# First-layer weights of the small expert slots: read from four fixed buffers instead of from a place looked up at run time

## The reference

```
xn  = layernorm(x)
out = x + scan(xn) + moe(xn)

scan: g, v, d = xn @ Wg + bg, xn @ Wv + bv, xn @ Wd + bd
      h[t] = (0.001 + 0.998 * sigmoid(d[t])) * h[t-1] + sigmoid(g[t]) * tanh(v[t])

moe:  scores = sigmoid(xn @ Wg.T + bg + bias)           # 8 experts
      the two best experts of each token, weighted by their scores
      expert(e) = gelu(xn @ W1[e].T + b1[e]) @ W2[e].T + b2[e]   # 256 -> 1024 -> 256
      shared    = gelu(xn @ Ws1.T + bs1) @ Ws2.T + bs2            # every token
```

## Time and profile before

| | |
|---|---|
| median of the runs | 710.67 us (710.16 to 711.31) |
| the profiled execution: its time | 710.67 us |
| its span, first to last instruction | 708.8 us |
| PE, share of the span busy | 94% |
| PE without a gap, big slots | 345 to 620 us |
| small slots on PE | about 651 to 698 us |
| granted TensorE clock, mean | 0.99 of full speed |

### The profile page before, as it was taken

One profiled execution on the slowest core, in us unless ns is written; L12 is line 12 of the kernel. 1 busy time (PEld: TensorE's weight loads), 2 busy tenths in 40 slices (PEclk: granted clock), 3 DMA queues, 4 the chain that ended last, 5 costly groups with the idle time before them and its releaser, 6 DMA issues.

```text
span 708.8 us, 20193 instructions
## 1 busy us (share of the span) xinstructions
PE 665.5 (94%) x5872; PEld 521.3 (74%) x5873; DVE 513.5 (72%) x1329; ACT 430.4 (61%) x738; POOL 285.4 (40%) x261
## 2 busy tenths in 40 slices
PE   4879999999999999699999999999999999999993
PEld 3455747565656565488988888888888888898773
DVE  5878989898989888766667666676666666666652
ACT  7967776868686855455555555555555555555651
POOL 2132332323242424234554645545446455463421
PEclk9999999999999999999999999999999999999997
DMA  7424334342516131222433323334333243332421
GB/s 258 169 71 139 90 120 112 97 137 71 172 57 182 35 120 31 70 44 60 67 52 61 67 53 66 57 60 66 55 60 66 53 67 54 61 65 50 72 40 23
DMA packets 54172, 57.55 MB, mean 81 GB/s; under 512 B 13204, under 2 KB 48916, under 8 KB 54136
## 3 DMA queue, kind: packets, MB, share of 16 engines
q1 hardware_dynamic: 38456, 38.42, 18.4%
q0 software_dynamic: 15680, 18.69, 16.4%
HBM read 38.53 MB, written 18.55 MB: 81 GB/s over the span
## 4 chain that ended last, share of the span: by engine, by line
PE 75%; DVE 13%; issue 5%; ACT 3%; DMA 2%; POOL 0%; DVEq 0%; SPq 0%; ACTq 0%; POOLq 0%
PE bank L1213 33%; PE bank L1205 29%; PE bank L1232 3%; PE bank L1193 3%; PE bank L1262 2%; PE bank L1244 2%; DVE W L800 2%; DVE arena L896 1%; DVE arena L839 1%; DVE arena L897 1%; PE bank L1184 1%; DVE arena L852 1%; DVE small L809 1%; DMA arena<-in_gates 1%; PE bank L1149 1%
## 5 line engine op out<-in xcount | busy, mean ns | idle before, releaser
L1213 PE MATMUL bank<-W,arena 128*128 (+1 forms) x2304 | 305.8, 274 | 16.0 <-DVE arena L897 14.0
L1205 PE MATMUL bank<-rows,W 128*128 128x256 f16 (+1 forms) x1920 | 299.2, 294 | 0.3 <-issue 0.2
L1213 PEld LDWEIGHTS bank<-W,arena 128*128 128x128 f16 x2304 | 222.4, 98 | 58.0 <-DVE arena L897 20.4
L1205 PEld LDWEIGHTS bank<-rows,W 128*128 (+1 forms) x1920 | 186.2, 98 | 54.5 <-issue 0.8
L592 ACT ACTIVATE arena<-bank,par 128x256 f32<-128x256 f32 x256 | 134.0, 559 | 80.3 <-PE bank L1205 69.3
L502 POOL DMA_INDIRECT out<-arena,slot_add x64 | 109.7, 1714 | 146.4 <-ACT arena L729 136.6
L896 DVE TENSOR_SCALAR arena<-arena,par 128x256 f16<-128x256 f32 x284 | 101.7, 358 | 81.7 <-ACT arena L592 54.8
L897 DVE SCALAR_TENSOR_TENSOR arena<-arena,par 128x256 f16<-128x256 f32 x284 | 138.7, 488 | 10.1
L438 POOL DMA_INDIRECT lists<-entry,place x64 | 67.9, 1061 | 150.6 <-ACT arena L578 73.2
L487 POOL DMA_INDIRECT rows<-xhl_rows,slot_list x64 | 68.9, 1076 | 51.8 <-DMA slot_list<-lists 34.8
L600 ACT ACTIVATE rows<-bank 128x1024 f16<-128x1024 f16 x32 | 32.7, 1023 | 60.9 <-PE bank L1262 33.4
(11 more groups left out here) (157 smaller groups left out, 519.9 us busy)
## 6 DMA issues: line engine op xcount, KB each, us to landing
stage<-in_w SPq DMA_DIRECT2D x32, 512.0 KB
b2row<-in_b SPq DMA_DIRECT2D x39, 128.0 KB
arena<-in_x SPq DMA_DIRECT2D x8, 512.0 KB
xhl_rows<-W SPq DMA_DIRECT2D x8, 512.0 KB
out<-arena SPq DMA_DIRECT2D x8, 512.0 KB
W<-in_w SPq DMA_DIRECT2D x4, 512.0 KB, 9.3
lists<-entry,place POOLq DMA_INDIRECT x64
rows<-xhl_rows,slot_list POOLq DMA_INDIRECT x64
```

The source lines that it names most:

```text
L1205: ins = T.matmul(bank_, weights(w, wp * HALF + c * H + j * P, P), rhs[:, 2 * xp + c, :], start=n == 0, stop=n == 3 * KD - 1)
L1213: ins = T.matmul(banks[t // 2][:, (t % 2) * D:(t % 2 + 1) * D], h[:, hp, t * P:(t + 1) * P], weights(w, (2 + wp) * HALF + j * D, D), start ...
```

## The change

SP copies the first layer's weights (both halves, 8 KB in each of 128 partitions, 1 MB) of each small slot from `W` to one of four buffers within SBUF: the two `stage` buffers and two pieces of `arena`. The seven copies go to the buffers in turn. The first four are started by SP after its work on slots 28 to 31; the other three after its work on slots 32, 33 and 34, each when PE has ended the first layer of the small slot that used the buffer before. `pair1` takes its weights from these buffers, whose addresses are fixed numbers; before its first matmuls of a slot it waits for the copy. `pair2` and the big slots are as they were.

```diff
+        small_w1 = [h[:, :].bitcast(F16) for h in (stage[0], stage[1], arena[:, 3072:5120], arena[:, 5120:7168])]
...
+        w1_in = [sem(f"w1_in{i}") for i in range(DEEP)]
...
+            def small_weights(m):
+
+                if m == 0:
+                    for l in range(2):
+                        for part in range(2):
+                            sp.wait_ge(stage_used[l][part], NW)
+                    sp.wait_ge(r_ok, 2 * SEQS)
+                    sp.wait_ge(o_out, 16 * SEQS)
+                if m >= DEEP:
+                    sp.wait_ge(ev_ps, EV_B + (m - DEEP + 1) * PAIRS)
+                s = sp.value_load(slot_set[0:1, BIG + m:BIG + m + 1], min_val=0, max_val=NW - 1)
+                sp.dma_start(small_w1[m % DEEP], W[:, bass.ds(s * WSET, 2 * HALF)]).then_inc(w1_in[m % DEEP], 16)
...
                 slot(n, n % 2)
                 if n < BIG - 8 + SMALL:
                     early_list(n + 8)
+                if n >= BIG - DEEP:
+                    small_weights(n - (BIG - DEEP))
             for n in range(BIG, SLOTS):
                 slot(n, n % 2)
+                if n + DEEP < SLOTS:
+                    small_weights(n - BIG + DEEP)
...
-            def pair1(ev, k, rhs, w):
-
-                pe.wait_ge(ev_act, ev + 1)
+            def pair1(m, k):
+
+                pe.wait_ge(ev_act, EV_B + m * PAIRS + k + 1)
+                if k == 0:
+                    pe.wait_ge(w1_in[m % DEEP], m // DEEP * 16 + 16)
                 for jj in range(2):
                     for n in range(3 * KD):
                         c, (wp, xp) = n // 3, PASSES[n % 3]
-                        ins = T.matmul(ps_e[k][:, jj * SROWS:(jj + 1) * SROWS],
-                                       weights(w, wp * HALF + c * H + (2 * k + jj) * P, P), rhs[:, 2 * xp + c, :],
-                                       start=n == 0, stop=n == 3 * KD - 1)
+                        o = wp * HALF + c * H + (2 * k + jj) * P
+                        ins = T.matmul(ps_e[k][:, jj * SROWS:(jj + 1) * SROWS], small_w1[m % DEEP][:, o:o + P],
+                                       xgT_small[m % DEEP][:, 2 * xp + c, :], start=n == 0, stop=n == 3 * KD - 1)
                 ins.then_inc(ev_ps, 1)
```

More of the change, by code:

```diff
@@ L1267, in first_layer @@
                 if is_small(n):
-                    pair1(EV_B + (n - BIG) * PAIRS + i, i, xgT_small[(n - BIG) % DEEP], w)
+                    pair1(n - BIG, i)
                 else:
```

## The result

The changed kernel takes 705.42 us, the median of four runs between 704.81 and 706.30, against 710.94 (710.16 to 711.31) for the kernel before beside it: a ratio of 0.9925, 95% interval 0.9908 to 0.9942. Measured again later beside other kernels it takes 705.01 us, a ratio of 0.9916 (0.9904 to 0.9929). The forecast was 705.1 in a range of 702.0 to 710.0. The profiled execution has a span of 703.8 us against 708.8.

What follows compares the result with a forecast made beforehand. PE bounds the kernel, in small slots through its sequencer's address instructions. Terms: -8.1 (addresses) + 0.4 (last addition) + 1.8 (copies in big slots) + 0.3 (bias row) = -5.6 from 710.67, so 705.1 us, range 702.0 to 710.0.

Steps and rivals of the forecast that it cites:

- Address instructions: In small slots 33 to 38, removing pair1's eight address instructions takes PE's work from 39.83 to 31.69 us, 8.1 us less.
- my bounds of 6.4 and 8.9: Gain in small slots 33 to 38: 6.4 us with idle gaps at slot starts as before, 8.9 with none.
- Rival 5: In small slots, pair1's pace stays because something other than address instructions sets it: 713.2 us, chance 0.05.
- rival 4: PE's sequencer spaces fixed-address matmuls at 67 ns, so pair1 in small slots takes 0.80 us: 707.8 us, chance 0.05.
- rival 3: The chain of gelu, split and scales look-up, not PE, sets small slots at 6.2 us or more: 707.6 us, chance 0.10.
- The last addition: At the kernel's end, slot 37's addition ends later against PE's end: 0.4 us lost, between 0 and 0.5.
- The copies in big slots: Lists queued behind copies delay gathers, so PE stands still at the turnings of slots 29 to 31: 1.8 us lost.
- D = 4.4 us: Assumed time for one 1.05 MB copy within SBUF, near the mean of 2.6 and 6.2 us.
- my own formula: PE's stall at turnings: D - 3.4 for slot 29, D - 4.0 each for slots 30 and 31, D being copy time.
- slack of 2.8 us: At slot 29's turning, rows land at 607.8 and PE turns them at 610.59, hiding 2.8 us of gather delay.
- Rival 1 and 2: Slow copies: 5.3 to 6.2 us sharing engines, 710.0, chance 0.14; or 7.6 us at half pace, 715.4, chance 0.08.
- The bias row in small slots: The next slot's b2row stands behind a copy on SP, so ACT waits a little: 0.3 us, between 0 and 2.

## Why the prediction was right, step by step

**Address instructions: right.** I forecast 31.69 us in place of 39.83 for slots 33 to 38, and 0.3 more for the bias row; measured are 31.84. Fixed addresses alone give 31.20, 8.6 us less, within my bounds of 6.4 and 8.9. Rival 5 (pace unchanged) and rival 4 (a floor of 67 ns; 0.67 / 12 = 56 ns was measured) are out. Slot 32 gains nothing, as said: its last pair2 still waits 0.70 us for the split.

**DVE and ACT as the next limit (rival 3): out.** A slot takes 5.7 us on average, with DVE 22.65 and ACT 21.11 us busy in 31.84; with fixed addresses alone PE is busy for 31.14 of 31.20.

**The last addition: right.** 0.4 forecast, 0.5 measured, and for the reason given: slot 37's addition starts 0.46 us later against the end of PE's work, and slot 38's waits for it.

**The copies in big slots: the size right, by luck in part.** 1.8 forecast, 1.7 measured, and the experiment with copies alone confirms about 2. But I had it all at the turnings. I took D = 4.4 us for a copy; the packets of the first four last 3.0 to 3.4 us (the row from start to landing says 5.0):

```profile
stage<-W SPq DMA_DIRECT2D x4, 1024.0 KB, 5.0
```

By my own formula D = 3.0 would have given nothing. The gather of slot 29 was late by 3.3 us all the same (forecast 3.8), because errors made up for each other in part: the copy's packets last 1.4 us less than I took, but the first comes 1.69 us after the start (600.21 to 601.90) and not 0.95, and the start itself is 0.15 later. The 2.34 us from the end of the copy to the gather were right. That SP starts the list 2.1 us later, since starting the copy takes 0.55 us and its look-up meanwhile 0.9 instead of 0.3, isn't what counts: where the list was started earlier (transfers from DRAM, copies in ACT's queue) the gather still comes 2.2 to 2.4 us after the end of the packets. With the slack of 2.8 us that I had read, 3.3 leaves 0.5; matmul by matmul PE lost 0.43 there. The other two turnings cost nothing; I had 0.4 for each.

The remaining 1.3 us stand elsewhere. 1.1 of it are delays in layer1 soon after the turnings (0.27, 0.46, 0.36), behind PE's own look-up of 0.86 to 1.06 us. 0.18 come later in slot 28, behind that slot's second look-up, which is short (0.31 us) but finds the sequencer 0.7 us behind; why it is behind there isn't shown. The look-up's step was missing: I asked what stands in the copy's queue, not which instructions read SBUF while it runs. With the copy behind the list, PE's look-ups are short and these delays are gone, though an addition is late instead; with the copy behind both and held back (timed), all of it is gone, 0.0 to 0.2 us.

**Rival 1 and 2 (a slow copy): out.** A copy's 310 to 350 GB/s is more than the 277 that I took from the loads. That a small transfer can't pass a large one, which I had placed in one queue alone, holds between queues as well: an addition of POOL's queue and a list of SP's queue both waited for a copy in another. The Trainium skill, "DMA: Bandwidth & Descriptors", section "Queues, rings and completion order", says that a DMA engine goes round its queues but works off a whole packet, of some 9 to 17 descriptors, before it changes. The eight pieces of 8 KB that a copy has for each of 16 engines fit that, and the trace agrees with the delay: in another queue the list's first packet comes at 602.43, when the copy's last are on their way (until 602.33).

**The bias row in small slots: right in size.** 0.3 forecast; ACT waited twice, 2.5 us at most, and slots 33 to 38 take 0.6 us more than without copies, in which PE's long look-ups (0.65 and 1.03 us there) have a share that isn't separated. That the row is sensitive to what SP does ahead of it is shown by the split copies (2.03 us of idle PE).

**Sum.** Forecast -5.6, measured -5.5 and -6.3 by the medians. The large term and its mechanism are right; that the term for the big slots agrees is partly luck, as said.

## What to carry to other kernels

If an engine's sequencer makes addresses between small matmuls, count its instructions against the array's time, and give it fixed addresses by moving the data; 8 instructions of 46 ns in a group of 12 matmuls made it 0.93 us long instead of 0.67. Before you start a big transfer out of SBUF in the background, list what reads single values out of SBUF meanwhile and which small transfers, in any queue, are due while it lasts, and start it just behind them: the same copies cost 2.3 us in one place and 0 to 1 us in another. Don't split it to let others through if the engine that starts the pieces has something else to start behind them.

## What the runs showed of the hardware

- A register's look-up out of SBUF (TENSOR_LOAD) mostly takes 0.30 us on PE (up to 0.49 without a copy), and 0.54 to 1.06 us while 1 MB is copied within SBUF in the changed kernel; with transfers from SBUF to DRAM up to 1.18 us, with transfers of the same size from DRAM to SBUF 0.3, once 0.54. In the kernel before, SP has one of 0.86 us while `out<-arena` goes from SBUF to DRAM. The Trainium skill, "SBUF — State Buffer", section "SBUF: two separate sides", says that engine ports and DMA ports can't contend. For the matmuls the runs agree: groups of pair1 and pair2 follow each other in 0.65 to 0.67 us during a copy (655.77, 656.43, 657.10, 657.75, with packets from 655.79 to 659.08) as without. The look-ups are held up by transfers that read SBUF, so for them the rule doesn't hold, or they don't go by the engine's ports; no run here tells which.
- A copy of 1 MB within SBUF in pieces of 8 KB has its packets on the way for 3.0 to 3.4 us, some 310 to 350 GB/s (the first five; the last two, beside additions and bias rows, up to 4.8 us); in pieces of 2 KB the first took 4.1 us.
- A transfer or an addition of another queue is served when the copy's packets are through: 1.6 us late for a 2 KB list, 1.8 us of waiting for an addition.
- In the changed kernel starting a 1 MB copy takes SP 0.50 to 0.55 us (0.33 to 0.35 for the small transfers); with split copies, four starts take 2.5 to 3.3 us.
